# Moving rotated q and k into score rows through DRAM scratch instead of by 32-row moves, with all q and k weights issued earlier

## The reference, cut to what matters

```python
q = (hidden_states @ Wq.T).reshape(b, s, H, HD).transpose(0, 2, 1, 3)
k = (hidden_states @ Wk.T).reshape(b, s, KVH, HD).transpose(0, 2, 1, 3)
v = (hidden_states @ Wv.T).reshape(b, s, KVH, HD).transpose(0, 2, 1, 3)
apply_rope = lambda x: x * cos + _rotate_half(x) * sin
q, k = apply_rope(q), apply_rope(k)
k, v = jnp.repeat(k, groups, axis=1), jnp.repeat(v, groups, axis=1)
logits = jnp.einsum('bhqd,bhkd->bhqk', q, k) * scale
attn = jax.nn.softmax(jnp.where(causal, logits, jnp.finfo(dtype).min), axis=-1)
out = jnp.einsum('bhqk,bhkd->bhqd', attn, v)
out = out.transpose(0, 2, 1, 3).reshape(b, s, H * HD) @ Wo.T
```

## Time and profile before

| | us |
|---|---|
| median of 3 runs (545.29 to 548.01) | 546.08 |
| the profiled execution | 547.53 |
| its span, first to last instruction | 545.70 |
| PE busy | 419.2 (77%) |
| DVE busy | 366.1 (67%) |
| ACT busy | 272.0 (50%) |
| POOL busy | 154.5 (28%) |
| mean granted TensorE clock | 0.891 |

### The profile page before, as it was taken

One profiled execution on the slowest core, in us unless ns is written; L12 is line 12 of the kernel. 1 busy time (PEld: TensorE's weight loads), 2 busy tenths in 40 slices (PEclk: granted clock), 3 DMA queues, 4 the chain that ended last, 5 costly groups with the idle time before them and its releaser, 6 DMA issues.

```text
span 545.7 us, 7590 instructions
## 1 busy us (share of the span) xinstructions
PE 419.2 (77%) x2604; PEld 328.9 (60%) x2636; DVE 366.1 (67%) x485; ACT 272.0 (50%) x779; POOL 154.5 (28%) x106
## 2 busy tenths in 40 slices
PE   3729480936869599696988979978998895459996
PEld 1523360725656477585777768857886783336774
DVE  2863232437898987589778848859785899855542
ACT  2214733506637465463667647647555575423321
POOL 2620000000263525133433423522242353311000
PEclk9867876868878989799999979999999998769999
DMA  8323213842134223230422233142113320000000
GB/s 201 64 65 94 52 30 72 225 125 84 35 96 132 81 94 86 74 97 19 129 76 58 50 115 97 32 136 92 29 37 121 97 69 29 0 1 13 21 21 25
DMA packets 53157, 40.62 MB, mean 74 GB/s; under 512 B 32280, under 2 KB 47840, under 8 KB 53120
## 3 DMA queue, kind: packets, MB, share of 16 engines
q1 hardware_dynamic: 51232, 39.21, 26.5%
q10 hardware_dynamic: 1888, 0.94, 0.6%
HBM read 26.36 MB, written 1.18 MB: 50 GB/s over the span
## 4 chain that ended last, share of the span: by engine, by line
PE 33%; SPq 18%; DVE 18%; issue 15%; DMA 7%; POOL 6%; ACT 3%; DVEq 0%; POOLq 0%
SPq L286 6%; PE ps_p L1015 6%; PE ps_s L1027 6%; SPq L297 5%; PE ps_p L1229 4%; POOL rc L411 4%; DVE state L780 4%; PE ps_s L1214 4%; PE ps_p L1127 3%; DVE nmax L698 3%; DMA qt<-rc 3%; DVE state L773 3%; PE ps_r L1081 2%; PE ps_o L1109 2%; DMA kt<-rc 2%
## 5 line engine op out<-in xcount | busy, mean ns | idle before, releaser
L483 ACT ACTIVATE prob<-ps_s,nmax 128x256 f32<-128x256 f32 (+1 forms) x256 | 104.8, 444 | 77.6 <-DVE nmax L698 77.6
L417 POOL TENSOR_TENSOR y<-y,state 128x1024 f32<-128x1024 f32 x32 | 80.4, 2512 | 167.1 <-DVE state L786 167.1
L411 POOL TENSOR_TENSOR rc<-rc,rs 128x512 f32<-128x512 f32 x40 | 57.2, 1431 | 150.4 <-DVE rs L686 104.3
L1015 PE MATMUL ps_p<-xt_all,wq 128*128 128x256 f32 x256 | 74.2, 440 | 28.8 <-DMA wq<-wqkv_t 20.4
L698 DVE TENSOR_REDUCE nmax<-ps_s 128x2 f32<-128x512 f32 (+1 forms) x96 | 60.3, 683 | 53.3 <-PE ps_s L1038 53.3
L489 ACT ACTIVATE pt<-ps_r 128x512 f32<-128x512 f32 x96 | 53.9, 593 | 77.4 <-PE ps_r L1081 73.8
L1027 PE MATMUL ps_s<-kt,qt 64*128 64x256 f32 (+1 forms) x512 | 57.2, 368 | 36.2 <-DMA qt<-rc 36.2
L780 DVE TENSOR_TENSOR_SCAN state<-decay,state 128x1024 f32<-128x1024 f32 x32 | 81.5, 2546 | 2.3 <-ACT decay L509 1.2
L1015 PEld LDWEIGHTS ps_p<-xt_all,wq 128*128 128x128 f32 x256 | 53.0, 217 | 43.5 <-issue 25.5
L1027 PEld LDWEIGHTS ps_s<-kt,qt 64*128 64x128 f32 x512 | 48.6, 207 | 44.1 <-DMA qt<-rc 38.2
L1127 PE MATMUL ps_p<-wo,attn_t 128*128 128x256 f32 x256 | 62.3, 391 | 8.0 <-DVE x L803 4.1
(11 more groups left out here) (109 smaller groups left out, 508.8 us busy)
## 6 DMA issues: line engine op xcount, KB each, us to landing
bc<-bc_scratch SPq DMA_DIRECT2D x32, 512.0 KB, 4.8
qt<-rc SPq DMA_DIRECT2D x256, 32.0 KB, 1.8
wq<-wqkv_t SPq DMA_DIRECT2D x32, 64.0 KB, 2.5
kt<-rc SPq DMA_DIRECT2D x64, 32.0 KB, 1.8
kt<-kt SPq DMA_DIRECT2D x8, 256.0 KB, 3.0
wo<-wo_t SPq DMA_DIRECT2D x1, 2048.0 KB, 9.3
xs<-x SPq DMA_DIRECT2D x1, 1024.0 KB, 7.6
out<-x SPq DMA_DIRECT2D x4, 256.0 KB, 2.1
```

What stands on the lines that cost most here:

```text
L411: nc.gpsimd.tensor_tensor(rc[:, r % 2, :, :], rc[:, r % 2, :, :], rs[:], ALU.add).then_inc(rope_add, 1)
L417: nc.gpsimd.tensor_tensor(y[:, v % 2, :], y[:, v % 2, :], state[:, v % 2, :], ALU.add).then_inc(state_free, 1)
L483: nc.scalar.activation(o, i, ACT.Exp, bias=nmax[:, r, c:c + 1], accum_out=rsum[:, r, GRP + head:GRP + head + 1]).then_inc(exp_done, 1)
L1015: last = nc.tensor.matmul(o, lhs, rhs, start=(k == 0), stop=(k == KT - 1))
```

## The change

q and k no longer go directly from rc to qt and kt. For each q, SP writes rc to a DRAM scratch by two DMAs (one for each half of the heads, 128 rows of 1 KB each), waits until both have landed, and reads the scratch into qt by one DMA of 256 KB. For each k it writes by two DMAs in the same way, and reads by two DMAs of 256 KB, one for the lower and one for the upper 64 partitions. DVE's rope waits for the writes only, no longer for the rows to be in qt or kt. At the start the order is store k, store q, fetch k, fetch q.

The weights wq of heads 2 and 3 are issued on ACT's queue, behind ACT's other loads and ahead of its first activation. The second half of wk and wq of heads 4 and 5 are issued by SP after move_q(1), wq of heads 6 and 7 after move_q(2). wo and the FFN's weights stay between move_k(1) and move_q(4).

```diff
+        q_scr = nc.dram_tensor("q_scratch", (2, GRP * HD, S), F32, kind="Internal").ap()
+        k_scr = nc.dram_tensor("k_scratch", (2, KG * HD, S), F32, kind="Internal").ap()
...
-                load_wq(2)
...
+            def store(scr, f, done):
+
+                r = ROPE_AT[f]
                 sp.wait_ge(rope_add, r + 1)
+                for c in range(2):
+                    sp.dma_start(scr.rearrange("(h two i) s -> two h i s", two=2, i=HALF)[c], rc[:, r % 2, c, :]
+                                 ).then_inc(done, 16)
+
+            def store_q(u):
+
+                if u >= 2:
+                    sp.wait_ge(q_in[u % 2], 16 * (u // 2))
+                store(q_scr[u % 2], ("q", u), q_out[u % 2])
+
+            def store_k(j):
+
+                if j >= 2:
+                    sp.wait_ge(k_in[j % 2], 32 * (j // 2))
+                store(k_scr[j % 2], ("k", j), k_out[j % 2])
+
+            def fetch_q(u):
+
+                sp.wait_ge(q_out[u % 2], 32 * (u // 2 + 1))
                 if u >= 2:
                     sp.wait_ge(score_done, 3 * (u - 1))
-                for h in range(GRP):
-                    for c in range(2):
-                        to = (h % 2) * HD + c * HALF
-                        sp.dma_start(qt[to:to + HALF, u % 2, h // 2, :], rc[h * HALF:(h + 1) * HALF, r % 2, c, :]
-                                     ).then_inc(q_in[u % 2], 16)
...
+                sp.dma_start(qt[:, u % 2, :, :], q_scr[u % 2].rearrange("(a p) s -> p a s", p=P)
+                             ).then_inc(q_in[u % 2], 16)
+
+            def fetch_k(j):
+
+                sp.wait_ge(k_out[j % 2], 32 * (j // 2 + 1))
                 if j >= 2:
                     sp.wait_ge(score_done, 3 * KG * (j - 1))
-                for i in range(KG):
-                    for c in range(2):
-                        sp.dma_start(kt[c * HALF:(c + 1) * HALF, j % 2, i, :],
-                                     rc[i * HALF:(i + 1) * HALF, r % 2, c, :]).then_inc(k_half[j % 2], 16)
-                sp.wait_ge(k_half[j % 2], 16 * k_moves * (j // 2 + 1))
-                sp.dma_start(kt[HD:P, j % 2, :, :], kt[0:HD, j % 2, :, :]).then_inc(k_in[j % 2], 16)
-
-            move_k(0)
-            move_q(0)
+                for o in range(2):
+                    sp.dma_start(kt[o * HD:(o + 1) * HD, j % 2, :, :],
+                                 k_scr[j % 2].rearrange("(a p) s -> p a s", p=HD)).then_inc(k_in[j % 2], 16)
...
+            store_k(0)
+            store_q(0)
+            fetch_k(0)
+            fetch_q(0)
             move_q(1)
+            with nc.allow_non_contiguous_dma(reason="weights by the halves of a head, once"):
+                load_wk(1)
+            load_wq(sp, 4)
+            load_wq(sp, 5)
...
             move_q(2)
-            with nc.allow_non_contiguous_dma(reason="weights by the halves of a head, once"):
-                load_wk(1)
-                load_wq(3)
+            load_wq(sp, 6)
+            load_wq(sp, 7)
             move_q(3)
             move_k(1)
-            with nc.allow_non_contiguous_dma(reason="weights by the halves of a head, once"):
-                for g in range(4, KVH):
-                    load_wq(g)
...
+            load_wq(nc.scalar, 2)
+            load_wq(nc.scalar, 3)
...
-                        dve.wait_ge(q_in[i % 2], 16 * q_moves * (i // 2 + 1))
+                        dve.wait_ge(q_out[i % 2], 32 * (i // 2 + 1))
                     else:
-                        dve.wait_ge(k_half[i % 2], 16 * k_moves * (i // 2 + 1))
+                        dve.wait_ge(k_out[i % 2], 32 * (i // 2 + 1))
```

More of the change, by code:

```diff
@@ L189, in decoder_layer @@
         q_in = [sem(f"q_in{r}") for r in range(2)]
-        k_half = [sem(f"k_half{r}") for r in range(2)]
+        q_out = [sem(f"q_out{r}") for r in range(2)]
+        k_out = [sem(f"k_out{r}") for r in range(2)]
         k_in = [sem(f"k_in{r}") for r in range(2)]
@@ L240, in decoder_layer, with load_wq @@
         x2lo_done = sem("x2lo_done")
-        q_moves, k_moves = 2 * GRP, 2 * KG
+        w_k = wqkv_t[:, :, GRP * HD:(GRP + 1) * HD].rearrange("(k p) (j g) (two i) -> k j two p g i", k=KT, j=2, two=2)
+        w_q = wqkv_t[:, :, 0:GRP * HD].rearrange("(k p) g (h two i) -> k g two p h i", k=KT, two=2, i=HALF)
+        def load_wq(queue, g):
+            with nc.allow_non_contiguous_dma(reason="weights by the halves of a head, once"):
+                for k in range(KT):
+                    for c in range(2):
+                        queue.dma_start(wq[:, k, g, c, :].rearrange("p (h i) -> p h i", i=HALF), w_q[k, g, c]
+                                        ).then_inc(wq_in[g], 16)
+        q_scr = nc.dram_tensor("q_scratch", (2, GRP * HD, S), F32, kind="Internal").ap()
+        k_scr = nc.dram_tensor("k_scratch", (2, KG * HD, S), F32, kind="Internal").ap()
         block = ctx.enter_context(nc.Block())
@@ L259, in load_wk @@
                                          ).then_inc(wk_in[j], 16)
-                def load_wq(g):
-                    for k in range(KT):
-                        for c in range(2):
-                            sp.dma_start(wq[:, k, g, c, :].rearrange("p (h i) -> p h i", i=HALF), w_q[k, g, c]
-                                         ).then_inc(wq_in[g], 16)
                 load_wk(0)
-                load_wq(0)
-                load_wq(1)
+                load_wq(sp, 0)
+                load_wq(sp, 1)
                 for k in range(KT):
@@ L274, in _ @@
                 sp.dma_start(dtproj[:], dtproj_t).then_inc(ssm_in, 16)
-                load_wq(2)
-            def move_q(u):
-                r = ROPE_AT["q", u]
+            def store(scr, f, done):
+                r = ROPE_AT[f]
                 sp.wait_ge(rope_add, r + 1)
+                for c in range(2):
+                    sp.dma_start(scr.rearrange("(h two i) s -> two h i s", two=2, i=HALF)[c], rc[:, r % 2, c, :]
[4 more added lines that the diff above has]
+                store(q_scr[u % 2], ("q", u), q_out[u % 2])
@@ L289, in move_k @@
-            def move_k(j):
-                r = ROPE_AT["k", j]
-                sp.wait_ge(rope_add, r + 1)
+                sp.dma_start(qt[:, u % 2, :, :], q_scr[u % 2].rearrange("(a p) s -> p a s", p=P)
+                             ).then_inc(q_in[u % 2], 16)
+            def fetch_k(j):
+                sp.wait_ge(k_out[j % 2], 32 * (j // 2 + 1))
                 if j >= 2:
                     sp.wait_ge(score_done, 3 * KG * (j - 1))
-                for i in range(KG):
-                    for c in range(2):
-                        sp.dma_start(kt[c * HALF:(c + 1) * HALF, j % 2, i, :],
-                                     rc[i * HALF:(i + 1) * HALF, r % 2, c, :]).then_inc(k_half[j % 2], 16)
-                sp.wait_ge(k_half[j % 2], 16 * k_moves * (j // 2 + 1))
-                sp.dma_start(kt[HD:P, j % 2, :, :], kt[0:HD, j % 2, :, :]).then_inc(k_in[j % 2], 16)
@@ L302, in _, with move_q, move_k @@
-            move_k(0)
-            move_q(0)
+                for o in range(2):
+                    sp.dma_start(kt[o * HD:(o + 1) * HD, j % 2, :, :],
+                                 k_scr[j % 2].rearrange("(a p) s -> p a s", p=HD)).then_inc(k_in[j % 2], 16)
+            def move_q(u):
+                store_q(u)
+                fetch_q(u)
+            def move_k(j):
+                store_k(j)
+                fetch_k(j)
+            store_k(0)
+            store_q(0)
+            fetch_k(0)
@@ L1020, in scores @@
                 r, j = u % 2, u // KG
-                pe.wait_ge(q_in[r], 16 * q_moves * (u // 2 + 1))
-                pe.wait_ge(k_in[j % 2], 16 * (j // 2 + 1))
+                pe.wait_ge(q_in[r], 16 * (u // 2 + 1))
+                pe.wait_ge(k_in[j % 2], 32 * (j // 2 + 1))
                 def dot(bank, col, h, t, keys, start=False):
```

## The result

| | before | changed |
|---|---|---|
| median of 4 runs | 546.61 us (545.29 to 548.01) | 559.50 us (557.81 to 561.97) |
| profiled execution, its span | 547.5 us, 545.7 us | 557.81 us, 556.0 us |

The ratio of the times is 1.0239 (95% interval 1.0191 to 1.0288): the changed kernel is 13 us slower. The prediction was 539 us, faster, with a range of 520 to 553 us. It was wrong in sign, and the time lies outside the range.

What follows compares the result with a forecast made beforehand. SP's load order bounds the kernel to 132 us, then a loop through DVE, PE and ACT. Terms -20.5 + 8 + 3 + 1 + 1.2 = -7.3 us from 547.5 us give 540.2 us; predicted median 539 us, range 520 to 553 us.

Steps and rivals of the forecast that it cites:

- the head: The run up to unit 4's scores, claimed to get 20.5 us shorter.
- The count of engines: Stores of q and k: four heads outermost, so each store runs on 4 DMA engines.
- The pair's 4.4 us: Two stores of one q or k: 3.0 us of data and 1.35 us other, landing after 4.4 us.
- First scores, -2.8 us: At the start, q0 in place at 36.5 us instead of 39.27 us.
- ACT's loads, +0.9 us (0 to 2): At the start, eight loads ahead of ACT's table load make POOL's rstd 0.9 us late.
- rival 3: ACT's loads delay the start more, the 12.2 us FFN block grows: 3 to 6 us less head gain, 544 us; chance 0.10.
- Unit 4's scores, at 98.5 us for 119.0: After k1's add at 72.8 us: k's 5.5 us, FFN block 12.2 us, q's trip 7.1 us, 0.9 us more.
- The groups, +8 us and +3 us of clock: Five later groups' beginnings: q 1.6 us later each behind k and bc, +8 us; two waits reach half clock, +3 us.
- Single units, +2.2 us: Units with little time for q's 7.1 us trip: five cost +1 us, units 8 and 9 +1.2 us.
- rival 2: Every unit's scores: q's trip outgrows its 7 us; decides from 7.5 us, 564 us at 8.5 us; chance 0.20.
- the sign named for this: Among the signs of being wrong: a pair of stores takes over 5 us.
- the bound of 5.3 us: High end for a pair of stores, if 256 KB took as long as bc; the groups then cost +15 us.

Runs made afterwards that it cites:

- scratch alone: The changed kernel with all weights loaded in the order of the kernel before, only q and k through the scratch: 570.8 us, ratio 1.0479.
- bc behind q, with the scratch: Changed kernel with early weights all by SP, FFN's loads behind q4 and q5, bc behind the next q, stores of 32 rows: 501.0 us, ratio 0.9216.
- the kernel with 32-row moves: Kernel before with early weights all by SP, and wo and the FFN's loads behind q4 and q5: 524.4 us, ratio 0.9631.

## Why the prediction was wrong, by its steps

Between the two profiled executions the sum was off by 17.6 us (+10.3 for -7.3). Of this 5.1 us are the head, 9.1 the groups with their clock, and 3.5 the single units. The step that failed most is the groups' term, +8 us and +3 us of clock, which measured +20.1 us: it had the bulk in front of q's store end too early. The mechanisms were right, all three terms were too favourable, and together they turned the sign.

- **The count of engines: right.** A pair is 264 packets, and 8 of them close it; the earlier trace rows was enough to read four engines off. **The pair's 4.4 us: 0.4 us too small.** 256 KB at the measured 101 GB/s are 2.6 us, less than the 3.0 of the sum; it is the start and the end, which I had from a write on 16 engines, that are longer. The fetch took 2.7 us, as forecast. The trip of q was thus 7.6 us (q2's add ended at 60.14 us, its scores began at 67.77), not 7.1.
- **First scores, -2.8 us: -2.0.** From k0's add to the scores it is 11.3 us (29.09 to 40.36), before 13.2. The scratch alone shows the same.
- **ACT's loads, +0.9 us (0 to 2): wrong, +3.1 us.** k0's add ended at 29.09 instead of 26.03 us. The eight loads took 0.88 us each, and with the table load behind them POOL's rstd came 2.2 us late. The rest goes with the x operations of DVE, 5.71 us for 4.60. Here rival 3 was right: it gave 3 to 6 us less gain at the head, and 5.1 came.
- **Unit 4's scores, at 98.5 us for 119.0: measured 103.57, so -15.4 for -20.5.** The cause was right: moving the FFN's block takes this wait away. But it was 13.4 us long, where some 9 were named. Of the 5.1 us that are missing, 3.7 are k1's add (76.5 us, not 72.8; 3.0 of them were there at the first scores), 0.7 is k's part of SP's queue (6.2 us, not 5.5) and 0.8 the block (13.0 us, not 12.2). The trip behind it was 7.9 us, as allowed for.
- **The groups, +8 us and +3 us of clock: wrong, +20.1 us; the mechanism held, its size did not.** q's narrow stores lie behind k and bc, as told. But the pair landed 16.3 us after k's add (249.34 to 265.64), not 14.1, and the scores came after 19.2 us, not 16.9. The waits in front of the five scores grew by 20.1 us, to 5.1 to 8.8 us each where 4 to 6 were named. The sum had let k's and bc's loads run from 5.3 to 10.5 us and put a full 3.6 us of store behind them. The DMA view of the changed kernel, 254 to 266 us (slices of 0.3 us), shows which of the two was too small:

```profile
GB/s 0 0 0 55 0 75 140 266 358 270 249 225 249 171 164 181 273 314 396 382 369 355 249 253 195 184 140 113 96 99 96 96 55 38 31 27 24 14 0 0
```

The traffic is above the pair's own level from 255.8 to 262.1 us, which is 6.4 to 12.8 us after k's add, and the pair is through 3.5 us after that. So the term that was too small is the end of the bulk, by 2.3 us: it began 1.1 us later, behind a store of 4.8 us and a longer start, and took 1.2 us longer than its 5.2. Issuing bc behind q takes 18.8 us out of the five ways, stores of 32 rows take 15.9 us: the bulk in front of the store and the few engines of the store each have a large part in what it costs. The 3 us of clock don't show as a term of their own: the waits' growth (20.1 us here, 5.7 us in the next step) is already the 25.7 us that everything behind the head cost.
- **Single units, +2.2 us: wrong, +5.7 us.** Units 8, 9, 10, 14, 22 and 31 wait 7.0 us together, before 1.25. A trip of 7.6 us, 0.5 us over the forecast, is past the 7.0 us of the earlier trace rows; in units 8, 9 and 10, which have half of these waits, bc and the up weights also stand on the queue.
- **The sum.** The head gave 15.4 us for 20.5; what came behind cost 25.7 us for 13.2. That is +10.3 us for -7.3.

So rival 2 came true, with its turning point: it put it at a trip of 7.5 us, and 7.6 us came. The price that it gave for this, 18 us for each us of trip, makes only 549 us at 7.6, because it took the landing behind bc to move by as much as the pair by itself; it moved by 2.2 us a group, the pair alone by 0.4. The rest of the miss is rival 3's, so two rivals that stood apart with 0.20 and 0.10 came together. What I had held against this rival, that a pair with nothing ahead of it has no reason for more than 4.4 us, was off by 0.4 us (4.8 us, so the sign named for this, a pair of over 5 us, shows only behind bulk), and most of the cost lies in pairs that have something ahead of them. With the bound of 5.3 us that the working itself named, the groups alone stood at +15 us, and the trip at 8.0 us, which at rival 2's price is 16 us more than the forecast, some 555 us; a range that ended at 553 us did not take this bound in.

Two things stay open. Behind the bulk the pair's last data, from 263.6 to 265.4 us, went at 14 to 55 GB/s and not at 101, so by the rate on fewer than four engines; why these came last, and how the loads and the store share their engines, no run shows. And DVE's eight x operations took longer the sooner POOL's convolution began behind their start: 5.71 us at 0.1 us (the changed kernel), 4.60 at 0.3 (the kernel before), 4.30 at 0.9 (bc behind q, with the scratch), 3.27 at 1.0 (heads 2 and 3 loaded by SP), and 2.67 us where it began after their end (scratch alone). This goes with the overlap of the two engines, but no experiment changed that overlap by itself, and 4.30 and 3.27 us at nearly the same offset are not explained. The Trainium skill ("SBUF — State Buffer", section "SBUF: two separate sides") has a rule of this kind: DVE, in a two-port mode or with two inputs from SBUF, and GpSimd take a shared pair of ports whole, and the later one blocks. The order of the five durations agrees with it; whether these x operations run in such a mode no run here shows.

## What to carry to other kernels

Look at the outermost count of both sides of a DMA: with four heads outermost a store had four engines, and the same bytes cut by head into rows made the kernel 25 us faster (ratio to the kernel before 0.9778 for 1.0239). Where a loop leaves a fixed time for a trip (here 7 us), a trip forecast right at it is not covered: every excess is paid in each round, so work out at which value the sum changes sign, and let the range reach to the bound of that term. And issue what is waited for next ahead of bulk that nobody waits for yet, with sixteen engines too: putting bc behind q took 10 us off the kernel with 32-row moves and 19 us off the one with narrow stores, and with stores of 32 rows and the FFN's loads spread as well, the kernel is 9% faster than the one before. Bulk that is moved as a whole lands in front of the next q (units 6 and 9 above), so move it in parts.

## What was new of the hardware

Loads on a compute engine's queue were not free to that engine: eight issues held ACT for 7.04 us, and the start came 3 us late. Such an issue took 0.82 to 0.88 us in the first 13 us of the run, on SP's queue in the kernel before just as on ACT's, and 0.54 us on SP's at 65 us (eight in 4.33 us). Two stores of 128 KB on four DMA engines each levelled off at 101 GB/s, four of 64 KB on two at 47. Cutting a store in four instead of two cost SP 0.7 us more of issue (1.73 for 1.06 us), and it landed 1.7 us sooner all the same, with sixteen engines on each part.
